# The hand-over from tokenizer to scan: three bias steps, one pair of products and nine unread products in another order

## What is computed

```python
h = tok(x)                       # 4x4 patches: mean + softmax(q.k) v, layer norms, projection
h = h + attn(layernorm(h))       # A = exp(-softplus(d)); u = (1 - A) * B * x; scan; y = C * s; y @ Wy + by
h = h + ffn(layernorm(h))        # 8 levels: score = <t, w1[node]> + b1[node]; choice = sign(score)
```

```python
def _layernorm(x, axis=-1, eps=1e-05):
    m = jnp.mean(x, axis=axis, keepdims=True)
    v = jnp.var(x, axis=axis, keepdims=True)
    return (x - m) / jnp.sqrt(v + eps)
```

## Time and profile before

| what | us |
|---|---|
| median of 3 runs | 612.56 (611.96 to 614.68) |
| the profiled execution, in all | 610.55 |
| its span (first to last instruction) | 608.8 |
| PE busy | 570.6 (94%) |
| DVE busy | 527.1 (87%) |
| ACT busy | 462.8 (76%) |
| POOL busy | 453.2 (74%) |

### The profile page before, as it was taken

One profiled execution on the slowest core, in us unless ns is written; L12 is line 12 of the kernel. 1 busy time (PEld: TensorE's weight loads), 2 busy tenths in 40 slices (PEclk: granted clock), 3 DMA queues, 4 the chain that ended last, 5 costly groups with the idle time before them and its releaser, 6 DMA issues. The chain is left out here.

```text
span 608.8 us, 16030 instructions
## 1 busy us (share of the span) xinstructions
PE 570.6 (94%) x5276; PEld 299.5 (49%) x5276; DVE 527.1 (87%) x1029; ACT 462.8 (76%) x968; POOL 453.2 (74%) x458
## 2 busy tenths in 40 slices
PE   6899999999999999999769999999869999999995
PEld 4222333232223333232235666666537888888884
DVE  3589999999999999999984899999988888888883
ACT  3898888888888888887355888888656777777772
POOL 6856998989988998876575157777777767667676
PEclk9999999999999999999999999999988999999998
DMA  7333333322233332100002994111123333322200
GB/s 266 160 136 140 140 139 139 135 73 86 125 139 139 139 139 86 66 11 2 15 0 83 233 210 109 50 45 40 40 70 108 82 83 85 77 70 73 70 18 1
DMA packets 49602, 58.19 MB, mean 96 GB/s; under 512 B 31932, under 2 KB 44836, under 8 KB 47544
## 3 DMA queue, kind: packets, MB, share of 16 engines
q1 hardware_dynamic: 44120, 49.23, 26.9%
q0 software_dynamic: 5120, 6.99, 3.5%
q10 hardware_dynamic: 288, 1.05, 0.4%
HBM read 50.19 MB, written 10.28 MB: 99 GB/s over the span
## 5 line engine op out<-in xcount | busy, mean ns | idle before, releaser
L872 PE MATMUL s_proj<-x_px,w_kv 64*64 64x512 f32 x256 | 129.4, 604 | 2.1 <-DVE qk L643 1.3
L876 PE MATMUL s_proj<-x_px,w_kv 64*64 64x512 f32 x256 | 130.5, 609 | 0.0
L2203 POOL DMA_INDIRECT out<-orow,m_rows x96 | 94.0, 979 | 41.1 <-issue 35.4
L1317 POOL DMA_INDIRECT rows_by_group<-r_pay,r_slot_i x64 | 73.5, 1148 | 32.3 <-DVE r_slot_i L1640 9.9
L528 POOL TENSOR_TENSOR half_px<-x_px 128x1024 f32<-128x1024 f32 x30 | 71.3, 2378 | 28.0 <-DMA x_px<-in_x 28.0
L549 POOL TENSOR_TENSOR pre<-va 128x1024 f32<-128x1024 f32 x32 | 76.2, 2381 | 21.2 <-DVE va L659 19.3
L643 DVE TENSOR_TENSOR qk<-s_proj,q 128x512 f32<-128x512 f32 x128 | 86.5, 677 | 3.8 <-ACT q L375 1.9
L659 DVE TENSOR_TENSOR va<-b_a,v_sb 128x1024 f32<-128x1024 f32 x62 | 75.6, 1220 | 5.4 <-PE b_a L906 5.3
L2172 PE MATMUL s_delta<-m_xsT,m_w_cur 128*64 128x128 f32 x1152 | 71.1, 273 | 0.0
L320 ACT ACTIVATE x_sq<-x_px 128x1024 f32<-128x1024 f32 x64 | 67.5, 1055 | 4.1 <-PE b_x L943 4.1
L903 PE MATMUL b_a<-a_sb,e_sw 64*64 64x512 f32 x124 | 63.9, 596 | 5.4 <-DVE va L659 3.5
(11 more groups left out here) (333 smaller groups left out, 1750.5 us busy)
## 6 DMA issues: line engine op xcount, KB each, us to landing
x_px<-in_x SPq DMA_DIRECT2D x15, 2048.0 KB, 7.8
m_rows<-rows_by_group SPq DMA_DIRECT2D x96, 72.0 KB
wt<-in_w2T SPq DMA_DIRECT2D x8, 512.0 KB
rows_by_group<-rows_by_group SPq DMA_DIRECT2D x1, 2286.0 KB, 9.7
out<-orow,m_rows POOLq DMA_INDIRECT x96, 2.3
x_px<-in_x ACTq DMA_DIRECT2D x2, 512.0 KB, 6.0
x_px<-in_x SPq DMA_DIRECT2D x2, 512.0 KB, 7.1
rows_by_group<-r_pay,r_slot_i POOLq DMA_INDIRECT x64
```

The costliest lines, as they stand in the source:

```text
L872: mm(b_k[i][HI, :], w_kv[LO, 0, :], px(t, j, LO), start=True, stop=True)
L876: mm(b_k[i][LO, :], w_kv[HI, 0, :], px(t, j, HI), start=True, stop=True).then_inc(done["kv_product"], 1)
L1317: g.indirect_dma_start(rows_d, bass.IndirectOffsetOnAxis(ap=slot_i[:, c % 2, k:k + 1], axis=0), pay[:, c % 2, k, :], None).then_inc(scatte ...
L2203: nc.gpsimd.indirect_dma_start(out_d, bass.IndirectOffsetOnAxis(ap=rows[:, i, ID0:ID0 + 1].bitcast(I32), axis=0), orow[:, i, :], None, bou ...
```

## The change

Three things move or come new; all of them are in the tokenizer block's drain.

```diff
@@ the VectorE loop
             if t == TILES + 1:
                 delta_limit()
                 normalise_first(0)
-                bias_parts()
             pool_last(t)
...
                 normalise_first(1)
                 scan_first()
                 normalise_first(2)
+                bias_parts()
@@ TensorE
+        def keep_busy(bank, times):
+
+            for _ in range(times):
+                mm(bank[:, 0:TOK], avg[:, :], h1[:, 0:TOK], start=True, stop=True)
+
...
-            if t > LAST_EARLY + 4 and t != TILES + 2:
+            if LAST_EARLY + 4 < t < TILES + 2:
                 out_mm(t - 4)
             kv(t - 1, 3)
             if t == TILES + 1:
                 centre_first(0)
+                pe.wait_ge(done["qk_ready"], NCH * TILES)
+                keep_busy(b_k[0], 1)
...
                 variance_first(2)
+                keep_busy(b_a[:, 0, :], 4)
...
             if t == TILES + 1:
                 variance_first(0)
+                keep_busy(b_k[0], 4)
...
         residual_first()
         delta_first(2)
+        out_mm(TILES - 1)
         inputs_second()
```

## The result

The changed kernel takes 605.4 us in the median (604.93 to 605.82, 4 runs), the kernel before 612.43 (611.96 to 614.68, 4 runs). The ratio is 0.9896, with a 95% interval of 0.9867 to 0.9926. That is 7.0 us less, where 5.5 us were forecast; 605.4 lies within the range. The profiled execution went from 610.55 to 605.56 us, 5.0 us less, with spans of 608.8 and 603.8 us. So three figures stand for one change, 7.0, 5.5 and 5.0, and the experiments have to say which is the kernel's.

What follows compares the result with a forecast made beforehand. The prediction took DVE's bias steps, then the wait for out_mm(15) and half-clock stretches, to bound the drain. -3.43 + 0.44 - 1.79 - 0.7 = -5.5 us, so 612.56 - 5.5 = 607.1 us; range 604.6 to 609.8.

Steps and rivals of the forecast that it cites:

- What bounded the drain: First half of the drain: bias steps on DVE delay va_mul(15, 0); without them va_mul(15, 3) comes 3.43 us earlier.
- POOL as the next bound: Ahead of spread(15, 3): out_mm(14) waits for POOL's fold of tile 14, ending at 305.79, so not all 3.8 us arrive.
- The scan gives something back: First scan on DVE: it sits through POOL's additions and takes 2.75 us, not 2.31; 0.44 us given back.
- mere sharing of speed: First scan, alternative: DVE and POOL share speed, the scan stays at 2.31 us, the sum 0.44 us better; no chance given.
- `residual_first` without `out_mm(15)` ahead: After the gate: residual_first no longer waits for POOL and two half-clock products; 1.79 us gained.
- The end chain at full clock: Residual to end of inputs_second on TensorE: 3.6 us at clock 1.00 instead of 4.29; 0.7 us gained.
- The bias steps in their new place: On DVE behind normalise_first(2): they take 2.2 us, between bounds of 1.5 and 4.83, ending at 317.5.
- DVE didn't become last: Rival at the join: bias steps of 4.83 us make DVE last; 609.0 to 610.9 us, chance 0.08.
- The rest stays as it is: Behind the join: the program keeps its length, so the whole 5.5 us reaches the end.
- slower than before: Rival, end of stage two: the half-clock stretch grows, each us costing half; 614.6 us with 15 us, chance 0.04.
- The clock: Drain: the products keep TensorE at 1.00; rival that it falls all the same, 1.6 us, 608.7 us, chance 0.14.
- more comes back: Rival in the drain: timed runs hold further half-clock stretches, 2.0 us, that go too; 605.1 us, chance 0.07.

Runs made afterwards that it cites:

- first-five kernel: The changed kernel without the last four of its nine products without a reader; the first five stay: 606.71 us in the median.
- e8: The changed kernel with spread(15, 3) moved ahead of centre_first(1) and out_mm(14): 605.18 us in the median.
- two-input edit: The changed kernel with the first scan's drive in PSUM and one product instead of four ahead of residual_first: 604.20 us, timed again 604.41.

## Why the prediction was right, step by step

- **What bounded the drain.** Right for the first half. With the bias steps gone `va_mul(15, 0)` starts 13.26 us after the drain's start and not 17.11. `va_mul(15, 3)` came 3.34 us earlier by the drain's clock (307.02 - 288.75 = 18.27 against 310.81 - 289.20 = 21.61), for 3.43.
- **POOL as the next bound.** Not what the trace shows, though the prediction names it as a sign of being wrong; that the number came out is luck. `spread(15, 3)` does stand behind `out_mm(14)`, but tile 14's fold had ended at 304.68 + 0.61 = 305.29, 0.15 us before `out_mm(14)` began, and a hand-over from POOL takes 0.06 (318.67 to 318.73 before). `out_mm(14)` began 0.63 us behind `centre_first(1)` (L987), which stands ahead of it on TensorE. It was the same 0.63 us before, with the fold done 3.44 us earlier, and in the first-five kernel, with the fold done 1.43 us earlier. TensorE's and POOL's timelines after:

```profile
304.81 0.70 PE L987 MATMUL s_ln<-h,cen 128*128 128x256 f32 x2
305.44 0.43 PE L977 MATMUL b_x<-pre,w_in 64*64 64x256 f32 x1
```

```profile
304.68 0.61 POOL L579 TENSOR_TENSOR pre<-pre 128x256 f32<-128x256 f32 x1
```

TensorE's before, where 309.23 follows:

```profile
308.60 0.70 PE L987 MATMUL s_ln<-h,cen 128*128 128x256 f32 x2
```

TensorE's and POOL's in the first-five kernel:

```profile
306.30 0.70 PE L987 MATMUL s_ln<-h,cen 128*128 128x256 f32 x2
306.93 0.43 PE L977 MATMUL b_x<-pre,w_in 64*64 64x256 f32 x1
```

```profile
304.89 0.61 POOL L579 TENSOR_TENSOR pre<-pre 128x256 f32<-128x256 f32 x1
```

From `spread(15, 0)` at 300.85 to the end of `spread(15, 3)` TensorE shows no wait after, and it was busy for 2.00 of 2.00 us in both windows from 302 to 306. So TensorE's own row of products set `va_mul(15, 3)`, and POOL's limit lay 0.1 us ahead of it. Bringing `spread(15, 3)` forward in that row (`e8`) moved `va_mul(15, 3)` by 0.92 us (17.35 us after the drain's start, against 18.27).

- **The scan gives something back.** Right in kind, too large: 2.58 - 2.31 = 0.27 us, for 0.44. The two-input edit shows the mechanism; without it the scan takes 1.26 us. The trace agrees with what the Trainium skill's page "SBUF — State Buffer" (Who interferes with whom) says of two SBUF inputs beside a GpSimd instruction that reads SBUF. It speaks against a mere sharing of speed that at another start the scan ended at the same time.
- **`residual_first` without `out_mm(15)` ahead.** Right: it starts 314.48 - 314.43 = 0.05 us behind the gate's end, so 1.79 us of waiting are gone. The four products ended ahead of it.
- **The end chain at full clock.** From the residual's start to the last product's end it took 318.26 - 314.48 = 3.78 us, for 3.6; the gain is 0.51 and not 0.7.
- **The bias steps in their new place.** 314.67 to 317.00, 2.33 us for 2.2 (4.83 before): four of the five take 0.29 to 0.48 us, with POOL done. DVE ended at 317.67, TensorE at 318.26, so DVE didn't become last.
- **Sum by the join.** -3.34 + 0.27 - 1.79 - 0.51 = -5.37, where the drain lost 5.35 and the forecast was -5.5.
- **The rest stays as it is.** This step was off by 0.80 us in the profiled execution. The rival that was to end slower than before named what the profiles go with (the half-clock stretch ends later in stage three): 0.80 us, where it would have needed over 5.5.
- **The clock.** The chances were too sure in one respect. I took the two falls of the profile before as the rule; across the profiles without products a fall comes and goes behind the same wait. The products make falls rarer; whether a wait that they cover can still bring one isn't shown, since no profile has it.
- **From the sum to the median.** Here luck helped. The 607.1 is the median of three runs of the kernel before, 2.0 us above its own profile, less 5.5. The measured 605.4 lies below the 606.0 to 608.2 that carried most of the chance, next to the 605.1 of the rival "more comes back"; the range held it because it took that rival in. That the first runs of the kernel before had more time at half clock than its profiled one would explain 7.0 us in place of 5.8, and the other 49 runs make it likely, but it isn't shown for these.

## What to carry to other kernels

An operation whose result is needed only in the next stage should stand in a wait of its engine behind the chain that ends the stage; look which engine is next on that chain, since it keeps a part of the gain (here TensorE's own row of products). The scan with both inputs in SBUF, beside a busy GpSimd, took 1.8 to 2.4 times as long as with one in PSUM (2.31 to 2.98 us against 1.26); putting one input into a free PSUM bank took 1.3 us off a 2.6 us step and gave GpSimd its own time back. Where single times spread by several us, work out each execution's time at half clock before crediting an edit with a difference of medians, and compare profiles by stretches between two instructions that every kernel has.

## What the runs showed of the hardware that was not expected

TensorE's clock fell behind waits of 1.85 to 3.28 us in some executions and stayed at its upper level behind waits of 1.85 to 2.04 us in others: 1.93 us ahead of tile 15's first spread brought a fall in the profiles before and with the bias steps alone, and none in the profile without products. Each of the kernel before's executions spent 15.8 to 28.2 us at half clock, and its time went from 610.3 to 612.2 with it in the median.
